# Two models on sixteen batches: the first model's first batches among the weight preparation, and one written-out order

## What is computed

```
# model 1, on each batch; (a1, g1, be1, a2, g2, be2) come from cond = [t, c] @ Wc + bc, Wc is 512 x 1536
h = layernorm(x) * (1 + g1) + be1
x = x + a1 * (softmax(Q K^T / 16) V)            # Q, K, V = h @ Wq + bq, h @ Wk + bk, h @ Wv + bv
h = layernorm(x) * (1 + g2) + be2
x = x + a2 * gelu(gelu(h @ W1 + b1) @ W2 + b2)  # 256 -> 1024 -> 256, exact gelu

# model 2; every linear layer is a bitlinear
def bitlinear(x, w, nw): xq = int8 steps of (rmsnorm(x) * nw); wq = clip(round(w / mean|w|), -1, 1) * mean|w|; return xq @ wq.T
h = bitlinear(silu(c), wa0); y = bitlinear(h, wa1); h = bitlinear(silu(y[:896]) * y[896:], wa2)
h = rmsnorm(bitlinear(h, wa3) + ba3) * wr
s1, sc1, g1, s2, sc2, g2 = split(bitlinear(h, wa4) + ba4, 6)     # six rows per batch; wa4 is 1536 x 1536
mx = layernorm(x) * (1 + sc1) + s1
i, f, g = bitlinear(mx, wi), sigmoid(bitlinear(mx, wf)), bitlinear(mx, wg)
o = scan over tokens of (o = f * o + silu(i) * (1 - f)); o = rmsnorm(o) * gn * silu(g)
x = x + g1 * bitlinear(o, wo)
my = layernorm(x) * (1 + sc2) + s2
x = x + g2 * bitlinear(silu(gate) * val, wm2)     # gate, val = split(bitlinear(my, wm1), 2)
```

## Time and profile before

| | before |
| --- | --- |
| time, median of 3 runs | 791.42 us (789.38 to 791.88) |
| the profiled execution: time, span | 789.95 us, 788.1 us |
| busy in it: PE, DVE, ACT, POOL | 628.5, 620.6, 568.3, 458.3 us |
| mean granted clock of TensorE | 0.912 |
| read from HBM, written | 47.10 MB, 4.33 MB |

### The profile page before, as it was taken

How to read it: one execution, slowest core, us unless ns; L and a number is a source line. 1 busy time by engine, 2 the same in 40 slices (tenths; PEclk the granted TensorE clock), 3 DMA queues, 4 the chain that set the end, 5 groups by cost and what they waited for, 6 DMA issues and landing times.

```text
span 788.1 us, 13091 instructions
## 1 busy us (share of the span) xinstructions
PE 628.5 (80%) x3560; PEld 487.7 (62%) x3588; DVE 620.6 (79%) x1432; ACT 568.3 (72%) x1206; POOL 458.3 (58%) x647
## 2 busy tenths in 40 slices
PE   0631336899899999999999999999999998874552
...
DVE  3779888223768999999899989998899889888653
ACT  1234670447689999898989999998989888774431
POOL 2203360213647686867767686867678586856623
PEclk9955579799999999999999999999999999985866
DMA  8495800111010101202021011112021010110100
...
DMA packets 17821, 51.96 MB, mean 66 GB/s; under 512 B 2880, under 2 KB 3712, under 8 KB 16880
## 3 DMA queue, kind: packets, MB, share of 16 engines
q1 hardware_dynamic: 17488, 50.92, 18.7%
...
HBM read 47.10 MB, written 4.33 MB: 65 GB/s over the span
## 4 chain that ended last, share of the span: by engine, by line
PE 58%; DVE 20%; issue 9%; POOL 5%; ACT 5%; DMA 2%; SPq 1%; DVEq 0%; POOLq 0%; ACTq 0%
PE bank L1346 15%; PE bank L1401 14%; PE bank L1339 7%; PE bank L1474 6%; PE bank L1326 5%; PE bank L1392 5%; DVE qa_dx L872 4%; PE bank L1318 2%; PE bank L1524 2%; PE bank L1489 2%; DVE arena L1138 2%; DVE qa_am L860 2%; DMA arena<-wo_dram 1%; POOL arena L512 1%; DVE arena L1009 1%
## 5 line engine op out<-in xcount | busy, mean ns | idle before, releaser
L1392 PE MATMUL bank<-arena,w 128*128 128x256 f32 x512 | 117.8, 379 | 0.0
L1401 PE MATMUL bank<-arena,w 128*128 128x256 f32 x512 | 116.7, 381 | 1.0 <-ACT arena L633 1.0
L1392 PEld LDWEIGHTS bank<-arena,w 128*128 128x128 f32 x512 | 96.1, 190 | 15.0
L1401 PEld LDWEIGHTS bank<-arena,w 128*128 128x128 f32 x512 | 94.9, 190 | 13.0 <-ACT arena L633 1.2
L1326 PE MATMUL bank<-ident,arena 128*128 128x128 f32 x448 | 66.9, 283 | 21.8 <-ACT arena L685 16.1
L1474 PE MATMUL bank<-tern_wm,qTm 128*128 128x512 bf16 x228 | 71.5, 403 | 15.1 <-ACT arena L707 6.2
L512 POOL TENSOR_TENSOR arena<-arena,row_nm 128x1024 f32<-128x1024 f32 x32 | 75.4, 2357 | 6.6 <-ACT junk_u L715 6.6
L1326 PEld LDWEIGHTS bank<-ident,arena 128*128 128x128 f32 x448 | 53.1, 145 | 35.1 <-issue 20.1
L694 ACT ACTIVATE arena<-arena,round_col,qa_qs 128x256 f32<-128x256 f32 x96 | 50.5, 592 | 22.4 <-DVE qa_qs L881 22.4
L1346 PE MATMUL bank<-arena 128*128 128x256 f32 x256 | 61.5, 383 | 3.1 <-DVE arena L899 3.1
L827 DVE BATCH_NORM_STATS2 ln_st<-arena 128x6 f32<-128x256 f32 x128 | 48.0, 417 | 18.1 <-POOL arena L502 11.7
...
## 6 DMA issues: line engine op xcount, KB each, us to landing
arena<-rows_d SPq DMA_DIRECT2D x32, 384.0 KB, 3.8
...
```

What stands on the lines that cost most here:

```text
L1392: last = te.matmul(bank[3 - q % 2][:, m * S:(m + 1) * S], w1[:, k, (2 * q + m) * P:(2 * q + m + 1) * P], h2T[:, k, :], start=k == 0, stop= ...
L1401: last = te.matmul(bank[3][:, c * S:(c + 1) * S], w2[:, k, c * P:(c + 1) * P], g[:, k, :], start=k == 0, stop=k == HC - 1)
```

## The change

- SCHEDULE, EARLY and the hardware loop give way to ORDER, one list of part:batch for the whole program; run_pipeline walks it on every engine without a loop. The counters in the waits are plain numbers.
- The preparation is cut into parts of the same kind (load_..., abs_ for the sums, sum and mean, round_, tern_, ada0 to ada5 for the steps of the conditioning vectors) and stands in ORDER between parts of batches 0 to 3 of model 1. Before ada5_y, the step that gives the modulation rows, stand batches 0 and 1 whole, batch 2 as far as up2, and batch 3 as far as exp. x3 becomes a ring of eight buffers.
- Conditioning: the weights of 48 matmuls are 128x128 pieces of Wc, and the 16 conditioning columns move; Wc is loaded in two halves, ahead of the other large loads. The copies and the 12 transposes go.
- wa0 to wa4 are no longer rounded and clipped. VectorE makes two 0/1 matrices of each, w * (1/mean) > 0.5 and w * (1/mean) < -0.5, and TensorE multiplies the vector with the first and its negative with the second, into the same bank. The other weights keep their three passes; GpSimd rounds wi, wf, wg, wo and wm2, ScalarE wm1.
- VectorE sums |w| of wa1, wm1 and one chunk of wa4, ScalarE all others.
- wa4 goes through seven places: chunks 0 to 11 are loaded for the sums, the last seven stay for the sign passes, and chunks 0 to 4 are loaded a second time. The sign matrices of a chunk stand in one of five places and above an earlier chunk.
- Buffers are laid out anew in the two arenas; nrow's rows are one tensor.

The diff, cut:

```diff
-SCHEDULE = [
...
+ORDER = """
+load_cond0 load_x:0 load_cond1 load_qkv load_g0 load_mlp load_x:1 ada_c ada0_sq ada0_z vec2 ada0_r cond_mm0 vec3
+ln1_moments:0 ada0_q ln1_rstd:0 ln1_norm:0 xn1T:0 cond_f0 hT:0 cond_mm1 rows0_turned cond_f1 load_g1 k_mm:0 abs_wa0
+rows0_copy abs_wa1 store_rows0 q_mm:0 qT:0 v_mm:0 kT:0 s_mm:0 ln1_moments:1 sum0 ln1_rstd:1 score_max:0 mean0 exp:0 tern_wa0
+ada0_T tern_wa1 ln1_norm:1 abs_wa2 load_rows0:0 load_rows0:1 row_sums:0 ada0_qT ada0_mm abs_wa3 ada0_y ada1_z xb:0 v:0
+probT_mm:0 load_x:2 load_a0 load_g3 ada1_sq load_wm1 load_g2 load_rows0:2 vec4 probT:0 ada1_r av_mm:0 ada1_q ln1_moments:2
+ada1_T x2:0 ln1_rstd:2 ada1_qT xn1T:1 xb:1 ln2_moments:0 sum1 hT:1 ln1_norm:2 mean1 load_x:3 k_mm:1 ln2_rstd:0 tern_wa2
+ada1_mm ln2_norm:0 tern_wa3 xn2T:0 ada1_gate q_mm:1 abs_wm1 load_a1 load_a2 load_a3 h2T:0 qT:1 up0:0 abs_wi up1:0 abs_wf
+g0:0 ada1_y v_mm:1 kT:1 g1:0 ada2_z up2:0 abs_wg ada2_sq abs_wo up3:0 v:1 ada2_r vec5 abs_wm2 ln1_moments:3 load_rows0:3
+s_mm:1 ada2_q ln1_rstd:3 g2:0 g3:0 abs_a0 down0:0 score_max:1 abs_a1 exp:1 ada2_T down1:0 ada2_qT abs_a2 row_sums:1 abs_a3
+ada2_mm gelu2:0 probT_mm:1 ada2_y ada3_z ada3_sq gate2:0 vec6 probT:1 ada3_r back:0 av_mm:1 x3:0 ada3_q x2:1 ada3_T ada3_qT
+xn1T:2 xb:2 ln2_moments:1 sum2 hT:2 ada3_mm ln1_norm:3 mean2 ln2_rstd:1 ln3_moments:0 round_wi ln2_norm:1 sum3 k_mm:2 ada3_y
+round_wf round_wg xn2T:1 round_wo q_mm:2 h2T:1 ln3_rstd:0 mean3 ada4_sq weight_steps round_wm2 up0:1 round_wm1 up1:1 kT:2
+ada4_r g0:1 tern_wm1 vec7 g1:1 up2:1 qT:2 up3:1 g2:1 tern_wi load_a4 load_a5 load_a6 load_a7 load_a8 load_a9 load_a10
+tern_wf s_mm:2 g3:1 ada4_y down0:1 ada5_sq tern_wg ada5_z abs_a4 ada5_r down1:1 load_a11 abs_a5 score_max:2 tern_wo exp:2
+tern_wm2 load_rows v_mm:2 gelu2:1 abs_a6 v:2 abs_a7 gate2:1 probT_mm:2 ada5_q back:1 probT:2 abs_a8 av_mm:2 abs_a9 x3:1
+ada5_T row_sums:2 ada5_qT abs_a10 x2:2 ln2_moments:2 xn1T:3 xb:3 hT:3 ln2_rstd:2 abs_a11 k_mm:3 ln2_norm:2 sum4 kT:3 q_mm:3
+mean4 negated_gn tern_b0 xn2T:2 qT:3 h2T:2 s_mm:3 tern_b1 ada5_b0 tern_b2 ada5_b1 tern_b3 up0:2 load_b7 ada5_b2 tern_b4 g0:2
+ada5_b3 load_b8 tern_b5 ada5_b4 load_b9 tern_b6 up1:2 load_b10 tern_b7 ada5_b5 g1:2 ada5_b6 load_b11 tern_b8 ada5_b7 tern_b9
+ada5_b8 up2:2 tern_b10 ada5_b9 g2:2 tern_b11 ada5_b10 score_max:3 ada5_b11 exp:3 up3:2 ada5_y v_mm:3 g3:2 row_sums:3
+store_rows1 v:3 down0:2 load_rows1:0 load_x:4 load_rows0:4 load_rows1:1 load_x:5 load_rows2:0 load_rows0:5 down1:2 mx_a:0
+mx_b:0 sq_a:0 z_i:0 probT_mm:3 gelu2:2 a_rstd:0 am_i:0 probT:3 gate2:2 av_mm:3 z_f:0 back:2 z_g:0 x2:3 am_f:0 am_g:0 x3:2
+scales_ifg:0 ln2_moments:3 round_i:0 round_f:0 qT_i:0 ln1_moments:4 ln2_rstd:3 round_g:0 qT_f:0 int_f:0 ln1_rstd:4 int_i:0
+ln2_norm:3 qT_g:0 yi:0 int_g:0 xn2T:3 si:0 yf:0 th:0 yg:0 h2T:3 fT_mm:0 forget:0 sg:0 up0:3 fT:0 sgg:0 ipT_mm:0 g0:3 up1:3
+scan:0 ln3_moments:1 ob:0 g1:3 up2:3 mx_a:1 sq_so:0 so_rstd:0 up3:3 g2:3 ln3_rstd:1 vv:0 mx_b:1 sq_o:0 z_o:0 g3:3 o_rstd:0
+am_o:0 sq_a:1 down0:3 z_i:1 quant_o:0 ln1_norm:4 a_rstd:1 am_i:1 qTo_mm:0 z_f:1 down1:3 int_o:0 z_g:1 am_f:1 am_g:1
+scales_ifg:1 yo:0 gelu2:3 gate_o:0 round_i:1 ln1_moments:5 x4:0 load_rows1:2 round_f:1 qT_i:1 gate2:3 round_g:1 qT_f:1
+ln4_moments:0 back:3 int_i:1 qT_g:1 x3:3 ln4_rstd:0 int_g:1 my_a:0 ln1_rstd:5 int_f:1 my_b:0 yi:1 yf:1 si:1 z_m:0 am_m:0
+sq_m:0 yg:1 th:1 m_rstd:0 sg:1 fT_mm:1 quant_m:0 fT:1 sgg:1 forget:1 ipT_mm:1 qTm_mm:0 scan:1 xn1T:4 int_m:0 hT:4 val0:0
+ln3_moments:2 ob:1 gates0:0 sq_so:1 q_mm:4 mx_a:2 silu0:0 so_rstd:1 ln3_rstd:2 k_mm:4 vv:1 qT:4 u0:0 sq_o:1 z_o:1 gates1:0
...
+"""
+RING = 8
...
-def run_pipeline(eng, parts, schedule, nb):
-    most = max(lag for _, lag in schedule)
-    def step(k, parity):
-        for name, lag in schedule:
-            if isinstance(k, int) and (not 0 <= k - lag < nb or k == lag and name in EARLY):
-                continue
-            if name in parts:
-                parts[name](Batch(k - lag, (parity + lag) % 2))
-    first = most + 2
-    first += (nb - first) % 2
-    for k in range(first):
-        step(k, k % 2)
-    with eng.Fori(first, nb - 1, 2) as i:
-        for w in range(2):
-            step(i + w, (first + w) % 2)
-    for k in range(nb, nb + most):
-        step(k, k % 2)
+    if value > 0:
+        eng.wait_ge(sems[b.p], value)
+def run_pipeline(eng, parts, order):
+    for entry in order.split():
+        name, _, i = entry.partition(":")
+        if name in parts:
+            parts[name](Batch(int(i or 0)))
...
+        SLOTS, WOVEN = 7, 5
...
+            def load_group(k, *after):
+                def part(_):
+                    for name, count in after:
+                        sp.wait_ge(s[name], count)
+                    for n in GROUPS[k]:
+                        if n != "wm1":
+                            load_weight(n, group_sems[k])
+                return part
+            def load_wm1(_):
+                sp.wait_ge(s["wtern"], TERNARY_ORDER.index("wa1") + 1)
+                load_weight("wm1", group_sems[3])
...
+            def load_first(i):
+                def part(_):
+                    if i == 0:
+                        sp.wait_ge(s["cond_mm"], 2)
+                    elif i < SLOTS:
+                        sp.wait_ge(s["wtern"], ROOM[i][1])
+                    else:
+                        summed(sp, f"a{i - SLOTS}")
+                    sp.dma_start(wa4_slot(i), t["wa4"][:, i * O6:(i + 1) * O6]).then_inc(slot_sems[i % SLOTS], 16)
+                return part
+            def load_again(i):
+                def part(_):
+                    sp.wait_ge(s["woven_used"], i + 2)
+                    sp.dma_start(second_place(SLOTS + i), t["wa4"][:, i * O6:(i + 1) * O6]).then_inc(slot_sems[KEPT[i] % SLOTS], 16)
+                return part
...
+            def store_rows1(_):
+                sp.wait_ge(s["ada_x"], len(LAYERS) + 1)
+                sp.dma_start(rows1_d[:, :], rows1_out[:, :]).then_inc(s["rows1_stored"], 16)
...
+                ve.tensor_tensor(x3[b.i % RING], halves(2), x2[b.p], ALU.add).then_inc(s["x3_ready"], 1)
...
-            def ternary(magic, count, out, place):
-                ternary_n[0] += 1
-                dve.wait_ge(magic, count)
-                ve.tensor_scalar(out, place, MAGIC, 1.0, ALU.subtract, ALU.min).then_inc(s["wclip"], 1)
-                dve.wait_ge(s["wclip"], ternary_n[0])
-                ve.tensor_scalar(out, out, -1.0, None, ALU.max).then_inc(s["wtern"], 1)
...
+            def ternary(n):
+                def signs(_):
+                    place, j = rounding_place(dve, n)
+                    if n[0] == "w":
+                        out, below = tern_of(n), BELOW[n]
+                    else:
+                        k = int(n[1:])
+                        out, below = wa4_ternary(k), wa4_below(k)
+                        if k >= WOVEN:
+                            dve.wait_ge(s["woven_used"], k - WOVEN + 1)
+                    ve.tensor_scalar(out, place, winv[:, j:j + 1], 0.5, ALU.mult, ALU.is_gt).then_inc(s["wclip"], 1)
+                    if n[0] == "b":
+                        dve.wait_ge(s["wtern"], len(TERNARY_ORDER) + k)
+                    ve.tensor_scalar(below, place, winv[:, j:j + 1], -0.5, ALU.mult, ALU.is_lt).then_inc(s["wtern"], 1)
...
+                    ve.tensor_scalar(minus_aqT[:, 0:KC * NB], turned, -1.0, None, ALU.mult)
...
+            def cond_mm(h):
+                def part(_):
+                    pe.wait_ge(s["feat_loaded"], 96)
+                    pe.wait_ge(s["qkv_loaded" if h else "cond_loaded"], 64 if h else 16)
+                    for m in range(3 * C * h, 3 * C * (h + 1)):
+                        for k in range(4):
+                            last = te.matmul(bank[5 - h][:, m * NB:(m + 1) * NB], wc[:, k, m * P:(m + 1) * P], tcT[:, k * NB:(k + 1) * NB],
+                                             start=k == 0, stop=k == 3)
+                    last.then_inc(s["cond_mm"], 1)
+                return part
...
+            def ada5_mm(n):
+                def part(_):
+                    k = SECOND[n]
+                    if n == 0:
+                        pe.wait_ge(s["ada_qT"], 5)
+                    pe.wait_ge(s["wtern"], len(TERNARY_ORDER) + n + 1)
+                    for j in range(3):
+                        out, cols = bank[COND_BANKS[j]][0:NB, :], slice(j * 512, (j + 1) * 512)
+                        te.matmul(out, aqT[:, k * NB:(k + 1) * NB], wa4_ternary(n)[:, cols], start=n == 0, stop=False)
+                        last = te.matmul(out, minus_aqT[:, k * NB:(k + 1) * NB], wa4_below(n)[:, cols],
+                                         start=False, stop=n == KC4 - 1)
+                    last.then_inc(s["woven_used"] if n < KC4 - 1 else s["ada_mm"], 1)
+                return part
```

(26 more changed lines are left out.)

1045 lines of the change are left out of this document (553 added, 492 removed), and 11 rows, old and new, of the table SCHEDULE.

## The result

The changed kernel takes 777.93 us (median of 4 runs, 776.76 to 778.65) against 790.4 of the kernel before, a ratio of 0.9844 (95% interval 0.9821 to 0.9867): 12.5 us faster, where 20.4 were forecast. The profiled execution has a span of 775.3 us, against 788.1.

What follows compares the result with a forecast made beforehand. The kernel loses time at its ends, the opening to waiting. q_mm:4 starts at 9.5 + 147 + 9.7 + 53 = 219.2, 18.7 earlier; with the loop 20.4, giving 769.6 profiled, median 771 us, range 749 to 796.

Steps and rivals of the forecast that it cites:

- Start, 9.5: Kernel head: TensorE can begin once the first half of Wc, 1.5 MB, has landed, at 9.5 us.
- TensorE's work, 135: Opening up to ada5_y: TensorE's work, old stretch plus woven-in batches, doubled sign-matrix matmuls and changed conditioning, sums to 135 us.
- Density, 92%: Opening up to ada5_y: TensorE busy 92%, as in the first model's own step, so its work takes 147 us.
- the blocked-queue rival: Weight chain before ada5_y: in-order waits hold TensorE at 74%, 34.5 us more, 806 us; decides under 81%; chance 0.13.
- ada5_y at 156.5: End of the opening: the second model's modulation rows due at 156.5 us.
- Hand-over 9.7, chain 53: Behind ada5_y: 9.7 us for it, its store and broadcast load; then 53 us from mx_a:0 to q_mm:4.
- "From q_mm:4 on the same parts": From q_mm:4 to the last store: both orders hold the same parts in the same sequence, engine by engine.
- Loop, 1.7: Periodic steps: writing out the looped steps takes 1.7 us off, straight-line code priced at nothing.
- Drain, no change: End of the kernel: the drain stays unchanged at 155.7 us.
- Sign passes, 0.95: wa4's 24 VectorE sign passes: 0.95 us each; rival with 1.74 each, 19 us more, 790 us, chance 0.07.
- GpSimd's chains, up to 10.6: Opening: seven rstd chains on GpSimd slowed beside VectorE's weight passes, 10.6 us if each is waited for; rival 782, chance 0.16.
- Dense opening, 750: Opening and following chain: TensorE 98% busy, chain 48.5 us, batches at full clock, 750 us; rival, chance 0.14.

Runs made afterwards that it cites:

- the three edits: Changed kernel with conditioning by rows (second form), wm1's means and clipping early, and the first conditioning layer's small steps ahead of wa1's sign passes: 762.3 us, ratio 0.9656.

## Why the prediction was right, and where it was off

The sign held, and the mechanism: from q_mm:5 to the last q matmul nothing gained or lost but the loop, and the change is decided by when the periodic part starts. By the span 12.8 us were gained of the 20.4. The misses, in us, add to 7.6: q_mm:4 4.6 late (223.75 for 219.2), the step behind it 1.3 long, the loop 0.4 short (1.3 in ten steps for 1.7), the drain 1.4 long. That q_mm:4 missed by 4.6 only is in part luck: TensorE had less work than was forecast and did it at a lower density, and the 135 us of the forecast at the density that was reached would have taken 9 us more. Two of the forecast's own signs of being wrong showed as well, a hole of 5.9 us behind sign passes and a periodic step of 37.0 us.

- **Start, 9.5**: 11.4. Batch 0's x and Wc's second half are issued 0.7 and 1.3 us behind the first half; that they share the transfer rate with it is the likely reason, which no run splits off.
- **TensorE's work, 135**: 127.4, and the terms were off by more than that, both ways. The 48 f32 matmuls leave 96 records with a weight load each, 20.7 us and not 9.1; the forecast's own row had shown 24 records for 12 such matmuls (L1521 to L1524: three banks, four pieces), which the text ahead of it counts as 24 matmuls. Against that wa4's 72 matmuls, 0.215 us apart, are 15.5 us, where the forecast has the old 36 as they were (12.1) and 8.8 more; batch 2's up3, which it counts, stands behind ada5_y (1.8); and most of the rest is that the first-model batches ran mostly at full clock, where they had been priced by a batch with q and k matmuls at half.
- **Density, 92%**: 84%, near the 81% at which the blocked-queue rival would have taken over. This is the step that failed most: 127.43 us of work at 92% are 138.5 us, it took 151.1. The longest hole is where a small step of the weight chain stands behind large passes in an in-order queue (5.9 us behind wa1's signs, closed by the run that moves the step), and 32.4 to 73 us has 13 of the 23.7 idle us. The first-model step that lent its 92% has no such chain. The other holes were not tried one by one.
- **ada5_y at 156.5**: 162.7. The last stage is VectorE's: 24 passes from 136.4 to 161.0 us, with TensorE's doubled matmuls beside them (one matmul less: 2.5 us).
- **Hand-over 9.7, chain 53**: 8.4 and 52.6.
- **"From q_mm:4 on the same parts"**: wrong by one step. From q_mm:5 on they are the same. Batch 3's MLP is already done at q_mm:4, so that step holds 24.8 us of TensorE's work, not 35; it takes 37.0 all the same, as the second model's chain sets it (10.6 of its 12.2 idle us are two waits for VectorE's steps of the second model).
- **Loop, 1.7**: the forecast counted a looped step (q_mm:6 to 7) among the written-out three and a written-out one (14 to 15) among the eight. Looped steps took 35.95, and 35.62 where nothing else is changed, so the loop costs 2.6. The changed kernel's steps take 35.74, 0.12 more than that; why, no run shows. **Drain, no change**: 157.1 for 155.7. Over the runs it is 155.6 to 157.4 with the same parts, at granted clocks of 0.79 to 0.82, so I take it for scatter; the run without the loop, which asked for it, left it open.
- **Sign passes, 0.95**: 1.02. Not 1.74; that rival is out.
- **GpSimd's chains, up to 10.6**: out by size, though its 782 is nearer to the measured time than 771. Seven power steps in the opening took 5.7 us together; five took 0.70 to 0.72 each, as in the earlier trace rows, and two, with the step behind each, were stretched by 1.9 us in all. The stretching itself is there, both ways: with wa0's pass it makes some 3 us of busy time. By the Trainium skill's page "SBUF — State Buffer", section "Who interferes with whom", one engine blocks the other for a whole instruction where both use the port pair that they share; the rows from 44.24 and 61.81 agree, since the later of the two ends only behind the earlier one. The forecast misread its own row: what ran beside the 2.23 us was not a weight pass but a pass of VectorE over two inputs of 16x1536 (L1225, 86.82 to 88.59 us); the step ended 0.6 us behind it.
- **Dense opening, 750**: not with this order, but 762.3 with the three edits shows that over half of the way from 778 was open.
